# First stacks by head halves in three attentions; first fetches and roots rearranged at the end of layer 3

## The reference

```
x = layernorm(x + attention_i(x)); x = layernorm(x + ffn_i(x))        # i = 0..3, eps 1e-5
attention 1: 16 heads of 8; softmax(-sqrt(max(|q|^2 + |k|^2 - 2 q.k, 1e-12))) v
attention 2: 16 heads of 8, grouped projections; softmax(q.k / sqrt(8)) v
attention 3: 16 heads of 8, causal; softmax(q.k / sqrt(8)) v
ffn 0: one expert of 8 with a capacity     ffn 1: two experts of 8, mean weight per expert
ffn 2: three layers of +-1 weights         ffn 3: two experts of 8 with a capacity (the largest weights),
                                                  gelu experts of width 256, a shared gelu expert of 512
layernorm(x) = (x - mean) / sqrt(variance + 1e-5)
```

## Time and profile before

| what | value |
|---|---|
| median of 3 runs | 2625.88 us (2622.5 to 2627.6) |
| the profiled execution | 2630.59 us |
| its span, first to last instruction | 2628.7 us |
| mean granted TensorE clock | 0.922 |
| busy: PE, DVE, ACT, POOL | 2271.8, 1547.5, 1562.8, 1324.9 us (86, 59, 59, 50%) |
| attention 1, first to last score | 855.9 to 1235.5 us |
| attention 2, first to last score | 1591.5 to 1850.6 us |
| attention 3, first to last score | 2101.9 to 2352.0 us |
| fetches of layer 3's end | 2528.1 to 2613.1 us |

### The profile page before, as it was taken

The page is one execution under the profiler, slowest core; times in us unless marked ns, Lnnn a source line. Parts: engine busy times, 40 slices in busy tenths (PEclk is TensorE's granted clock), DMA queues, the critical chain, the costliest instruction groups (busy, mean ns, idle before and its releaser), DMA issues. The chain is left out here.

```text
span 2628.7 us, 52174 instructions
## 1 busy us (share of the span) xinstructions
PE 2271.8 (86%) x17672; PEld 1613.1 (61%) x17672; DVE 1547.5 (59%) x4261; ACT 1562.8 (59%) x3796; POOL 1324.9 (50%) x2132
## 2 busy tenths in 40 slices
PE   6999999999385799998579967999699699997893
PEld 3666666666285466665369954666355367775792
DVE  3576766766621799999653326787300166655375
ACT  3666666666243699999345533787522247774362
POOL 2454545545253788884143236774100268862756
PEclk9999999999787699999779978999899899998995
DMA  4000000000321322220311214442000133311342
GB/s 167 1 1 1 1 1 1 1 1 1 106 65 54 98 65 81 72 65 25 114 53 50 46 46 122 116 114 84 9 0 0 37 110 103 99 55 45 100 144 78
DMA packets 106499, 153.36 MB, mean 58 GB/s; under 512 B 17330, under 2 KB 78660, under 8 KB 99204
## 3 DMA queue, kind: packets, MB, share of 16 engines
q1 hardware_dynamic: 93956, 127.24, 15.5%
q0 software_dynamic: 12288, 22.86, 3.5%
HBM read 100.87 MB, written 47.19 MB: 56 GB/s over the span
## 5 line engine op out<-in xcount | busy, mean ns | idle before, releaser
L181 POOL TENSOR_SCALAR A_prob<-A_prob,A_rinv 128x256 f32<-128x256 f32 x512 | 236.0, 480 | 342.8 <-DVE A_rinv L397 342.7
L993 DVE TENSOR_REDUCE A_nmax<-A_S 128x2 f32<-128x512 f32 (+1 forms) x512 | 311.5, 621 | 144.7 <-PE A_S L770 83.5
L922 ACT ACTIVATE A_PT<-A_E 128x512 f32<-128x512 f32 (+1 forms) x512 | 272.6, 550 | 121.3 <-PE A_E L788 63.2
L349 ACT ACTIVATE A_prob<-A_S,A_nmax 128x256 f32<-128x256 f32 x512 | 235.3, 478 | 4.6 <-DVE A_nmax L392 4.6
L392 DVE TENSOR_REDUCE A_nmax<-A_S 128x2 f32<-128x512 f32 x256 | 164.9, 686 | 93.6 <-PE A_S L268 93.6
L1867 POOL DMA_INDIRECT L_xe<-rows,L_index x112 | 106.5, 951 | 201.8 <-PE L_k L1958 88.3
L1590 DVE TENSOR_SCALAR_CACHE_REDUCE A_D<-A_S 128x256 f32<-128x256 f32 x512 | 193.7, 418 | 14.2 <-PE A_S L1373 13.9
L1596 DVE COPY A_PT<-A_T 128x512 f32<-128x512 f32 x256 | 175.2, 687 | 19.2 <-PE A_T L1386 18.8
L1386 PE MATMUL A_T<-ident_sb,A_D 128*128 128x128 f32 x1024 | 161.4, 281 | 27.2 <-ACT A_D L1515 14.6
L2013 PE MATMUL L_k<-L_w,L_hT 128*128 (+1 forms) x1216 | 167.2, 275 | 0.4 <-ACT L_hT L2159 0.3
L362 ACT ACTIVATE A_OT<-A_O,A_bv 128x256 f32<-128x256 f32 x128 | 60.7, 474 | 178.8 <-PE A_O L295 178.8
(11 more groups left out here) (413 smaller groups left out, 5995.0 us busy)
## 6 DMA issues: line engine op xcount, KB each, us to landing
A_QS<-stack_q SPq DMA_DIRECT2D x144, 192.0 KB
A_KS<-stack_k SPq DMA_DIRECT2D x144, 192.0 KB
results<-L_ye SPq DMA_DIRECT2D x48, 256.0 KB
stack_q<-A_parts SPq DMA_DIRECT2D x48, 192.0 KB
stack_k<-A_parts SPq DMA_DIRECT2D x48, 192.0 KB
L_w<-f_w SPq DMA_DIRECT2D x24, 256.0 KB, 6.7
sent<-A_zeros SPq DMA_DIRECT2D x10, 512.0 KB
L_xe<-sent SPq DMA_DIRECT2D x20, 256.0 KB
```

The source lines that it names most:

```text
L181: nc.gpsimd.tensor_scalar(prob[:, n % NP, j, t, :], prob[:, n % NP, j, t, :], rinv[:, n % NP, j, t:t + 1], 1.0, ALU.mult, ALU.mult).then_i ...
L349: nc.scalar.activation(prob[:, n % NP, j, t, :], psS[n % 2][j][:, t, :], ACT.Exp, bias=nmax[:, n % NP, j, t:t + 1], scale=1.0, accum_out=r ...
L922: nc.scalar.activation(PT[:, n % RING, :], psE[n % 2][:, 0:BLOCKS, :].rearrange("p a b -> p (a b)"), ACT.Exp, scale=scale).then_inc(expd, 1)
L993: nc.vector.tensor_reduce(nmax[:, b % 2, :, h], view, AX.X, ALU.max, negate=True).then_inc(maxed, 1)
```

## The change

In the three attentions the loads of batch 0's stack are issued twice, each for half of the heads: six transfers of 96 KB for heads 0 to 7, counted by a new semaphore `halved`, then six for heads 8 to 15, counted by stacked[0]. score(0) waits for halved, score(8) for stacked[0]. All other batches load as before.

At the end of layer 3 the fetches for k = 0 wait for h_psum of HALF + LAG + t = 42 + t instead of Q - NT + t = 48 + t. GpSimd computes no roots any more; its program ends with the 32 fetches for k = 1. ScalarE takes the square root of veps (root(g), behind its coefficient copies, with the table of the square root loaded before them), and VectorE makes the inverse by a reciprocal and one step of refinement, r (1.5 - 0.5 v r^2), in write(g).

```diff
# attention_small and, with the same lines, attention_dist: SyncE, stack(b)
+                    if b == 2:
+                        sp.wait_ge(halved, 96)
...
-                    for a in range(PARTS):
-                        rows = slice(a * PARTS * HD, (a + 1) * PARTS * HD)
-                        sp.dma_start(QS[rows, buf, :, :].rearrange("r h n -> r (h n)"),
-                                     scratch["q"][i].rearrange("a (c h) n -> (a c) (h n)", h=H)).then_inc(stacked[i], 16)
-                        sp.dma_start(KS[rows, buf, :, :].rearrange("r h n -> r (h n)"),
-                                     scratch["k"][i, a].rearrange("(c h) n -> c (h n)", h=H).unsqueeze(0).to_broadcast([PARTS, HD, H * SEQ])).then_inc(stacked[i], 16)
+                    for some, signal in [(slice(0, H * SEQ // 2), halved), (slice(H * SEQ // 2, H * SEQ), stacked[i])] if b == 0 else [(slice(0, H * SEQ), stacked[i])]:
+                        size = some.stop - some.start
+                        for a in range(PARTS):
+                            rows = slice(a * PARTS * HD, (a + 1) * PARTS * HD)
+                            sp.dma_start(QS[rows, buf, :, :].rearrange("r h n -> r (h n)")[:, some],
+                                         scratch["q"][i].rearrange("a (c h) n -> (a c) (h n)", h=H)[:, some]).then_inc(signal, 16)
+                            sp.dma_start(KS[rows, buf, :, :].rearrange("r h n -> r (h n)")[:, some],
+                                         scratch["k"][i, a].rearrange("(c h) n -> c (h n)", h=H)[:, some].unsqueeze(0).to_broadcast([PARTS, HD, size])).then_inc(signal, 16)
# TensorE, score(n); in attention_dist the waits for n2_in and filled stay at h == 0
-                    if h == 0:
+                    if n == 0:
+                        pe.wait_ge(halved, 96)
+                    if n == H // 2 or h == 0 and b:
                         pe.wait_ge(stacked[b % 2], 96 * (b // 2 + 1))
# routed_layer, GpSimd
-                if cap2:
-                    nc.gpsimd.memset(mhalf[:], -0.5).then_inc(filled, 1)
-                    pool.wait_ge(filled, 1)
...
                 for t in range(NT):
-                    pool.wait_ge(h_psum, Q - NT + t)
+                    pool.wait_ge(h_psum, HALF + LAG + t)
                     fetch(0, t)
                 for i in range(2):
                     pool.wait_ge(stored[i], 16 * len(range(i, NQ, 2)))
-                def root(g):
-                    s = slice(g * G, (g + 1) * G)
-                    pool.wait_ge(var_ready, g + 1)
-                    nc.gpsimd.tensor_tensor(rstd[:, s], veps[:, s], mhalf[:, s], ALU.pow).then_inc(rooted, 1)
-
-                for g in range(NG):
-                    for t in range(g * G, (g + 1) * G):
-                        fetch(1, t)
-                    if g >= 2:
-                        root(g - 2)
-                root(NG - 2)
-                root(NG - 1)
+                for t in range(NT):
+                    fetch(1, t)
# routed_layer, ScalarE
                 if cap2:
+                    nc.scalar.preload_act_table_set("sqrt_and_others")
                     for g in range(NG):
                         act.wait_ge(coefT_psum, g + 1)
                         nc.scalar.activation(coefT[...], psC[g % 2][0:E + 1, :], ACT.Copy).then_inc(coefT_out, 1)
+                def root(g):
+                    s = slice(g * G, (g + 1) * G)
+                    act.wait_ge(var_ready, g + 1)
+                    nc.scalar.activation(deviation[:, s], veps[:, s], ACT.Sqrt).then_inc(rooted, 1)
+
+                def write_out(g):
+                    act.wait_ge(shift_ready, 2 * g + 2)
+                    for t in range(g * G, (g + 1) * G):
+                        nc.scalar.activation(x_state[:, t, :], y[:, t, :], ACT.Identity, bias=shift[:, t:t + 1], scale=rstd[:, t:t + 1]).then_inc(written, 1)
+                if cap2:
+                    for g in range(NG):
+                        root(g)
+                        if g:
+                            write_out(g - 1)
+                    write_out(NG - 1)
# routed_layer, VectorE, write(g)
                     dve.wait_ge(rooted, g + 1)
+                    nc.vector.reciprocal(rstd[:, s], deviation[:, s]).then_inc(refined, 1)
+                    dve.wait_ge(refined, 3 * g + 1)
+                    nc.vector.scalar_tensor_tensor(out=deviation[:, s], in0=rstd[:, s], scalar=-0.5, in1=veps[:, s], op0=ALU.mult, op1=ALU.mult).then_inc(refined, 1)
+                    dve.wait_ge(refined, 3 * g + 2)
+                    nc.vector.tensor_tensor(deviation[:, s], deviation[:, s], rstd[:, s], ALU.mult).then_inc(refined, 1)
+                    dve.wait_ge(refined, 3 * g + 3)
+                    nc.vector.scalar_tensor_tensor(out=rstd[:, s], in0=deviation[:, s], scalar=1.5, in1=rstd[:, s], op0=ALU.add, op1=ALU.mult).then_inc(shift_ready, 1)
+                    dve.wait_ge(shift_ready, 2 * g + 1)
                     nc.vector.scalar_tensor_tensor(out=shift[:, s], in0=mv[:, s, 0], scalar=-1.0, in1=rstd[:, s], op0=ALU.mult, op1=ALU.mult).then_inc(shift_ready, 1)
```

More of the change, by code:

```diff
@@ L543, in attention_small @@
         xT_psum, xT_ready, qk_psum, qk_ready = sem("xT_psum"), sem("xT_ready"), sem("qk_psum"), sem("qk_ready")
-        v_psum, v_ready = sem("v_psum"), sem("v_ready")
+        v_psum, v_ready, halved = sem("v_psum"), sem("v_ready"), sem("halved")
         split, stored, stacked = sem("split"), [sem(f"stored{i}") for i in range(2)], [sem(f"stacked{i}") for i in range(2)]
@@ L1366, in score @@
                     q, k, S = QS[0:KR, b % NBUF, h, :], KS[0:KR, b % NBUF, h, :], psS[n % 2]
+                    if n == 0:
+                        pe.wait_ge(halved, 96)
+                    if n == H // 2 or h == 0 and b:
+                        pe.wait_ge(stacked[b % 2], 96 * (b // 2 + 1))
                     if h == 0:
-                        pe.wait_ge(stacked[b % 2], 96 * (b // 2 + 1))
                         pe.wait_ge(n2_in, 32 * (b + 1))
@@ L1733, in routed_layer @@
             stats, mv, shift = sb("stats", [P, NT, 6]), sb("mv", [P, NT, 2]), sb("shift", [P, NT])
-            veps, rstd, mhalf = sb("veps", [P, NT]), sb("rstd", [P, NT]), sb("mhalf", [P, NT])
+            veps, rstd, deviation = sb("veps", [P, NT]), sb("rstd", [P, NT]), sb("deviation", [P, NT])
         first_in, early = [], [(numbers[:], consts["numbers"].partition_broadcast(P))]
@@ L1785, in routed_layer @@
         fetched = [[sem(f"fetched{k}{g}") for g in range(NG)] for k in range(K)] if cap2 else None
-        stated, aggregated, var_ready, rooted, shift_ready = (
-            sem("stated"), sem("aggregated"), sem("var_ready"), sem("rooted"), sem("shift_ready"))
+        refined, stated, aggregated, var_ready, rooted, shift_ready = (
+            sem("refined"), sem("stated"), sem("aggregated"), sem("var_ready"), sem("rooted"), sem("shift_ready"))
         if cap2:
@@ L2168, in _ @@
                         nc.scalar.activation(coefT[:, 4 * g:4 * g + 4, :].rearrange("e t p -> e (t p)"), psC[g % 2][0:E + 1, :], ACT.Copy).then_inc(coefT_out, 1)
-                for g in range(NG if cap2 else 0):
-                    act.wait_ge(shift_ready, g + 1)
+                def root(g):
[4 more added lines that the diff above has]
+                    act.wait_ge(shift_ready, 2 * g + 2)
                     for t in range(g * G, (g + 1) * G):
                         nc.scalar.activation(x_state[:, t, :], y[:, t, :], ACT.Identity, bias=shift[:, t:t + 1], scale=rstd[:, t:t + 1]).then_inc(written, 1)
+                if cap2:
[4 more added lines that the diff above has]
+                    write_out(NG - 1)
             @block.vector
```

## The result

| | before | after |
|---|---|---|
| median | 2625.94 us (8 runs, 2622.13 to 2627.74) | 2615.47 us (8 runs, 2612.83 to 2619.54) |
| the profiled execution, its span | 2630.59, 2628.7 us | 2616.03, 2614.1 us |
| mean granted clock | 0.922 | 0.925 |

The ratio of the medians is 0.9966, 95% interval 0.9955 to 0.9977: 9 us faster by the ratio, 10.5 by the medians. The attentions were forecast at +2.1 us in sum and the end at -2.5; both gave more.

The account below looks back on a forecast made before the run. The prediction saw TensorE busy 86% of the span, over eight stages with different limits. It summed -2.5 (end) + 1.5 (clock) + 3 x 0.2 (attention starts) = -0.4 us: 2625.5 us from the median of 2625.88, range 2617 to 2632.

Parts of the forecast that it names:

- Roots off GpSimd: End of layer 3: last fetch issued 6.5 us sooner, but VectorE becomes the bound; gain 2.5 us, bounds 0 and 5.5.
- the wait for root 0: End of layer 3: VectorE's second round waits for ScalarE's first square root, behind the last coefficient copy, ready at 2586.0.
- the small operations' 1.0 us: End of layer 3: five chained small VectorE operations in a row take 1.0 us instead of 0.16.
- the table load hidden: After the last gelu: ScalarE's square-root table load costs 0; uncovered it would cost 1.3 us.
- the rounds: End of layer 3: each VectorE group of four fetches takes 5.4 us with refinement, 4.37 before.
- the end gives all it can: Rival, end of layer 3: root 0 not waited for, 5.5 us gained, layer 3's clock holds; 2620.4 us, chance 0.17.
- a start that carries through in one layer: Rival's one-layer case: an attention's earlier start carries through, 2617 us; chance 0.08 for the whole rival.
- Fetches begun sooner: End of layer 3: second fetches begin at 2567.4 against 2568.59, 1.2 us sooner, bounds 0 and 2.5.
- Attention 1: Layer 1's start: head 0 waits for the lengths instead of its stack; 0 gained, +0.2 us taken, bounds -5.27 and +3.
- Attentions 2 and 3, head 0 and head 16: Layers 2 and 3: head 0 some 5 to 8 us sooner, head 16 as before; 0.2 us lost per layer.
- the tail of K's broadcast: Attentions' stack loads: K's three-copy broadcast keeps two or three DMA engines busy some 6 us; halving leaves head 16 unmoved.
- The clock behind the longer wait: Attention 3, head 16 to the maxima's transpose: longer idling drops TensorE's clock, +1.5 us, bounds 0 and 2.3.

Follow-up runs that it names:

- end_only: The kernel before with only the end-of-layer-3 part of the change, stacks loaded whole: median 2615.42 us, ratio 0.9968.
- after_again: The changed kernel measured once more without any edit: median 2616.13 us, ratio 0.9962 to the kernel before.
- late_pool: The changed kernel plus a small GpSimd memset of an unread tile at the end, waiting for ScalarE's last write: median 2620.39 us.
- gate_back: The changed kernel with the first fetches' gate put back, to tile 48 on instead of 42 on: median 2618.68 us.
- halves_one_wait: The changed kernel with transfers still halved, but head 0 waiting for both halves: median 2617.67 us.
- whole_paced: The changed kernel with the first stack loaded whole, six 1.5 KB transfers put between the loads, and head 0 waiting for all: median 2618.46 us.

## Why the prediction was off, step by step

**Roots off GpSimd: the step that failed.** The forecast for the chain itself was -2.5 us. Measured from the last gelu to the last write it is -3.6 (end_only) and -3.9 (after_again). In it were right: the fetches' pitch without roots (1.265 forecast, 1.258), the wait for root 0 (by the prediction's steps from 2584.39 - 1.2 to 2586.0, 2.8 us; measured 2.65), VectorE as the bound, the small operations' 1.0 us (0.96), the table load hidden. Too dear were the rounds, 5.4 for 5.17 to 5.21 us, 0.9 us over four. But the sum ended at ScalarE's last write, as if what stands behind it, 7.3 us before, could not change: a term put at nothing without a reason. Before, 3.3 us behind SyncE's last landing were GpSimd's drain, since the last root was GpSimd's; that went with the roots. That term was worth 3.6 us, and late_pool shows it by bringing it back. The rival "the end gives all it can" had 5.5 us, and its reason, no wait for root 0, did not come true; the end gave 7 us with that wait in place. That the time still came within 1.5 us of the range is luck: its lower edge stood for a start that carries through in one layer, and none did.

**Fetches begun sooner.** Forecast -1.2 us. Shown by gate_back: 1.0. The first fetches began 2.5 us sooner, as forecast, counted from the last gelu (37.6 us ahead of it for 35.1). In the first profile of the changed kernel the gain was nothing, because the last stores landed later there; one execution would have misled.

**Attention 1.** Forecast: head 0 gains nothing, 0.2 us lost. Head 0 gained nothing. The next turn of x came 1.3 to 1.9 us sooner than before in eight of the nine profiles with these transfers (0.4 us in gate_back), by the gather of GpSimd's queue. I had looked only at the queue that the change edits, and at the waits for the stack, not at who else uses the same engines. Shown: the gather's wait goes with the halved transfers and not with the early head or the slower issue (halves_one_wait, whole_paced). Not shown: that the stage gains by it. From the turn of batch 1's x to the last score it took 390.0 to 393.0 us in the three profiles with whole rows, 389.9 to 393.5 in the nine with halves, in mean 391.9 and 390.5. A rule of the Trainium skill (DMA: Bandwidth & Descriptors, "Queues, rings and completion order") says that an engine takes turns between the queues it has work for, a packet at a time; that fits a gather that waits less behind 4 KB rows than behind 8 KB ones, and the runs don't show the engine's own order.

**Attentions 2 and 3, head 0 and head 16.** As forecast: head 0 6 to 8 and some 5 us sooner, head 16 nearly where it was. In attention 2 the seven profiles with this code have it at 37.2 to 38.9, in mean 37.9, the three with whole rows at 38.0 to 38.8, in mean 38.4; in attention 3 the seven have a mean of 33.9, the same three 34.3, 34.3 and 35.3, in mean 34.6. That is 0.5 and 0.7 us, less than the scatter of 1.7 and 1.0 us among equal code, whose cause is open. That head 16 hangs on the tail of K's broadcast was argued in the prediction and is shown now. With K's copies as three transfers head 16 came 3.4 to 5.5 us sooner. The rule of the Trainium skill that the prediction cited (DMA: Bandwidth & Descriptors, "Why a DMA increments its semaphore by 16 and not by 1") speaks for that too: 8 rows allow 8 engines where the leading 3 allows 3. The trace agrees in so far as the long 1s and 2s are gone; it does not say which engines carried the rows.

**The clock behind the longer wait.** Forecast +1.5 us in attention 3. The mechanism is shown: 5.65 us at 0.50 for 4.05 at 1.00, and halves_one_wait takes it away. The size on the path was wrong, for three reasons. First, the first head of the second pass had waited 1.80 us for the maxima before, and waits 0.74 now. It comes 46.7 us from the first split for 46.2, and the stage's last score is no later (291.8 us from the first split, for 292.3). Second, the clock had fallen before as well, only later: behind the wait of 1.80 us the second pass began at 0.51, and behind the one of 0.74 it stays at 1.00. The 3.4 us from there on, before and after:

```profile
2128.70:2132.10 3.40, 3.40 (x14) 1.86 (x13) 0.95 (x3) 0.86 (x2) 0.82 (x2) 0.51 0.16 58
```

```profile
2124.40:2127.80 3.40, 3.40 (x25) 2.23 (x26) 1.74 (x7) 0.98 (x2) 0.82 (x2) 1.00 0.15 53
```

Third, 4.05 us is not what whole rows always give: end_only and whole_paced waited 1.81 and 1.96 us at head 16 and took 5.1 us to the transpose. I had not looked for slack behind the transpose.

**The sum.** Forecast -2.5 (end), -1.2 within it, +1.5, +0.6 = -0.4 us. By the profiles: end -7.2 (-3.6 chain, -3.6 drain), shown by end_only and late_pool. The attentions' last scores come, in the mean of the profiles with halves against the three with whole rows, 1.4, 0.6 and 0.7 us sooner, each less than the scatter of equal code (up to 3.6 us in attention 1). That adds to -9.9, where after measured -10.5 and after_again -9.3; the agreement says little of the attentions' part. The two halves of the change measured -8.3 and -1.1. Of the 14.6 us between the two profiled executions, 3.5 are none of this: from the last score of attention 3's second pass to the last gelu, code that was not changed, the profile of before took 188.8 us, that of after 185.3, the twelve others 183.9 to 186.8. The forecast had set the profile of before 4.7 us over its median, and this is most of it. Why it took longer in that execution is open.

## What to carry to other kernels

Follow the path past the last useful instruction: ask at the end of a block which engine's drain ends last, and measure what a last small step on GpSimd costs there. Of a transfer that is changed, look at every queue that shares its engines, not only at its own. Follow a wait that is moved forward to the end of the stage: head 16 4.7 us sooner gave 1.5 us at the second pass and nothing at the last score, and with the same code in another kernel 5.5 us gave 4.9. A gain at the first slots is not yet a gain of the stage, and one profile of each kernel can't tell the two apart.

## What the runs showed of the hardware

- At the end of the last block GpSimd's drain ended 7.9 us behind the end of its last instruction, in fourteen profiles, after powers (before), after indirect fetches (after) and after a memset of 0.10 us (late_pool). SyncE's took 7 ns. At the ends of attentions 1 to 3 and of the routed layers 0 and 1 GpSimd's ended 1.4 to 6.9 us behind it (before).
- GpSimd's gather of 512-byte rows waited 5.9 to 6.3 us beside stack loads with 8 KB rows, 4.1 to 4.7 beside ones with 4 KB rows (one of 5.6), and with K's copies as three transfers 7.7 beside 8 KB rows and 3.1 beside 4 KB rows.
- Three transfers of 8 rows for one with a leading dimension of 3 took the stretch of 0.1 to 0.2 of the DMA engines away and brought head 16 3.4 to 5.5 us sooner.
- TensorE's work from head 16 to the transpose took 5.65 us at 0.50 (after) and 4.05 us at 1.00 (halves_one_wait).
- A square root of 128x4 on ScalarE took 0.19 to 0.21 us; five chained operations of 128x4 on VectorE 0.88 to 0.96 us, up to the start of the next (after).
